# Adding the first experts' output into a copy of x in DRAM instead of into x in SBUF, with three steps of the feed-forward in another order

## The reference

```python
# layer 0, "xattn": a mixture of experts, each token by its id to one of 4 experts
e = min(token_id // (25000 // 4), 3)
y = (silu(h @ ctx[e].T) * (h @ ctx[e].T)) @ ctx[e].T      # h = layernorm(x), ctx[e]: 512 x 512
x = x + tanh(g_xattn[0]) * y
# layer 0, "ffn": block-quantised activations and weights (blocks of 32, shared exponent)
x = x + tanh(g_ffn[0]) * mx_linear(silu(mx_linear(h, w_gate)) * mx_linear(h, w_up), w_down)   # 512 -> 2048 -> 512
# layer 1, "xattn": attention with 8 heads between layernorm(x) and ctx
x = x + tanh(g_xattn[1]) * attention(layernorm(x), ctx)
# layer 1, "ffn": router, 6 of 64 experts of width 192, and a shared expert
x = x + tanh(g_ffn[1]) * moe(layernorm(x))
```

## Time and profile before

| what | us |
|---|---|
| runs of the kernel before | 1041.68, 1046.04, 1039.69 (median 1041.68) |
| the profiled execution: its own time | 1041.68 |
| its span, first to last instruction | 1039.5 |
| experts of layer 0 (20 to 192): PE busy | 165.66 of 172 |
| seam (192 to 214): PE busy, granted clock | 10.49 of 22, 0.82 |
| feed-forward (214 to 408): PE busy | 179.13 of 194 |
| attention (408 to 630): PE busy | 215.39 of 222 |
| routing (630 to 700): PE busy | 65.23 of 70 |
| experts of layer 1 (700 to 1003): PE busy | 298.76 of 303 |

### The profile page before, as it was taken

The page is one execution under the profiler, slowest core; times in us unless marked ns, Lnnn a source line. Parts: engine busy times, 40 slices in busy tenths (PEclk is TensorE's granted clock), DMA queues, the critical chain, the costliest instruction groups (busy, mean ns, idle before and its releaser), DMA issues.

```text
span 1039.5 us, 13635 instructions
## 1 busy us (share of the span) xinstructions
PE 963.3 (93%) x4408; PEld 473.9 (46%) x4430; DVE 623.7 (60%) x1168; ACT 419.0 (40%) x817; POOL 632.1 (61%) x569
## 2 busy tenths in 40 slices
PE   6999999769999998899999999989999999999992
PEld 4454555334444444344444445335554555554530
DVE  5798977268888887677777778962222222222221
ACT  5565656134444444466666654331111111111100
POOL 4698975358888886786667651354554455444430
PEclk9999999989999999899999999999999999999997
DMA  8465431440000001500003405179999999999748
GB/s 274 158 205 195 152 122 71 91 91 1 1 1 1 2 1 41 195 29 21 21 21 86 177 1 203 61 265 296 345 344 338 338 341 341 336 340 333 181 61 186
DMA packets 64788, 162.90 MB, mean 157 GB/s; under 512 B 9760, under 2 KB 9904, under 8 KB 64336
## 3 DMA queue, kind: packets, MB, share of 16 engines
q1 hardware_dynamic: 47360, 116.94, 31.9%
q0 software_dynamic: 17360, 45.10, 18.3%
HBM read 129.67 MB, written 35.48 MB: 159 GB/s over the span
## 4 chain that ended last, share of the span: by engine, by line
PE 55%; POOL 8%; DVE 7%; issue 5%; DMA 3%; ACT 1%; DVEq 0%; POOLq 0%; ACTq 0%
PE PS L1590 15%; PE PS L1609 8%; PE PS L1434 6%; PE PS L1411 6%; PE PS L1422 6%; POOL ARENA L671 4%; PE PS L1579 3%; PE PS L368 3%; PE PS L1376 2%; PE PS L1395 2%; POOL ARENA L677 2%; DMA ARENA<-rows,idx 2%; DVE ARENA L1207 1%; DVE CT L1206 1%; DMA X<-gain 1%
## 5 line engine op out<-in xcount | busy, mean ns | idle before, releaser
L726 POOL TENSOR_TENSOR ARENA<-ARENA 128x512 f32<-128x512 f32 x128 | 133.1, 1061 | 55.5 <-DVE ARENA L1033 55.5
L772 POOL DMA_INDIRECT out<-ARENA,idx x32 | 45.8, 1430 | 127.3 <-DVE ARENA L1239 117.4
L1376 PE MATMUL PS<-SLAB,ARENA 128*128 128x512 bf16 x501 | 116.4, 382 | 3.3 <-ACT ARENA L1731 2.1
L1863 ACT ACTIVATE ARENA<-PS 96x192 f32<-96x192 f32 x64 | 20.9, 326 | 226.5 <-PE PS L1590 149.0
L1239 DVE COPY ARENA<-PS 96x512 f32<-96x512 f32 x64 | 41.1, 682 | 96.6 <-PE PS L1609 96.6
L1770 ACT ACTIVATE ARENA<-PS,ARENA 128x512 f32<-128x512 f32 x128 | 86.7, 682 | 22.8 <-DVE ARENA L1027 19.5
L1027 DVE TENSOR_REDUCE ARENA<-PS 128x2 f32<-128x1024 f32 x64 | 78.2, 1222 | 9.0 <-PE PS L1411 8.9
L1590 PE MATMUL PS<-SLAB,ARENA 128*96 128x384 f32 x240 | 81.0, 490 | 0.0
L1422 PEld LDWEIGHTS PS<-ident,ARENA 128*128 128x128 f32 x512 | 54.8, 141 | 51.1 <-issue 35.8
L1376 PEld LDWEIGHTS PS<-SLAB,ARENA 128*128 128x128 bf16 x512 | 49.6, 99 | 60.8 <-issue 4.8
L677 POOL TENSOR_TENSOR ARENA<-ARENA 128x1024 bf16<-128x1024 fp8e4 x32 | 61.1, 1909 | 24.6 <-DVE ARENA L998 24.5
(11 more groups left out here) (268 smaller groups left out, 1848.2 us busy)
## 6 DMA issues: line engine op xcount, KB each, us to landing
SLAB<-in_L_ffn_w_gate SPq DMA_DIRECT2D x30, 384.0 KB
SLAB<-in_L_ffn_w_up SPq DMA_DIRECT2D x30, 384.0 KB
X<-in_L_ffn_w_down SPq DMA_DIRECT2D x14, 768.0 KB
SLAB<-in_L_ffn_w_down SPq DMA_DIRECT2D x10, 768.0 KB
CT<-in_L_ffn_w_gate SPq DMA_DIRECT2D x16, 384.0 KB
CT<-in_L_ffn_w_up SPq DMA_DIRECT2D x16, 384.0 KB
X<-in_ctx SPq DMA_DIRECT2D x4, 1024.0 KB, 5.4
XNT<-in_L_ffn_w_gate SPq DMA_DIRECT2D x16, 256.0 KB
```

What stands on the lines that cost most here:

```text
L726: last = pool.tensor_tensor(prob[s % 4][:, h, :], prob[s % 4][:, h, :], rec[:, s % 4, h:h + 1].to_broadcast([P, D]), ALU.mult)
L1376: last = pe.matmul(bank(b), QT[:, par, k * P:(k + 1) * P], w[:, k, c * D:(c + 1) * D], start=(k == 0), stop=(k == KD - 1))
```

## The change

**1. Where x and y are added.** The DRAM tensor `gain` becomes `x_sum`. ACT copies x into it, DRAM to DRAM, by four DMAs of 1 MB, issued behind its second `normal_h`. The first scatter waits for these four copies (`x_in`), and every scatter now adds to what the rows of `x_sum` hold. SP's loads of x into `X` in slots 1 to 8 go, and so do POOL's four adding DMAs. Instead SP waits for all scatters and loads `X` tile by tile from `x_sum`, 16 plain DMAs of 256 KB, at most four under way; `enter(i)` waits for its own tile.

**2. POOL's step.** The scale and the offset are computed together (`deviation_x` now has all four operations), so in odd steps the offset's two come ahead of `normal_i(i, 0)` instead of behind it. `normal_h(i + 2)` comes ahead of `back_i(i, 0)` instead of behind it.

**3. DVE's step.** `cast_h` moves from behind the first two products of step i (tile i+1) to the end of the step before (there as tile i+2 of that step), and runs from step 0 on.

```diff
-    gain = nc.dram_tensor("gain", [T + SLOTS * P, D], F32, kind="Internal").ap()
+    x_sum = nc.dram_tensor("x_sum", [T + SLOTS * P, D], F32, kind="Internal").ap()
...
-        PARTS = ((0, 1), (1, 4), (4, 8), (8, NT))
...
                 for j in range(SLOTS):
                     if j in TILED and tile_at(j) + 2 < NT:
                         load_w(tile_at(j) + 2)
-                    if 1 <= j <= NT // 2:
-                        need(sp, c_turned, NT)
-                        sp.dma_start(X[:, 2 * j - 2:2 * j, :], x_v[:, 2 * j - 2:2 * j, :]).then_inc(x_in, 16)
+
+                sp.wait_ge(y_stored[0], 16 * ((SLOTS + 1) // 2))
+                sp.wait_ge(y_stored[1], 16 * (SLOTS // 2))
+                for i in range(NT):
+                    need(sp, yg_in[i % 4], 16 * (i // 4))
+                    sp.dma_start(X[:, i, :], x_sum_v[:, i, :]).then_inc(yg_in[i % 4], 16)
...
                 def scatter(j):
                     if j == 0:
                         pool.wait_ge(target_ready, 1)
+                        pool.wait_ge(x_in, 64)
                     pool.wait_ge(y_out, j + 1)
-                    pool.indirect_dma_start(gain, bass.IndirectOffsetOnAxis(ap=target[:, j:j + 1], axis=0),
-                                            ysb[:, j % 2, :], None).then_inc(y_stored[j % 2], 16)
+                    pool.indirect_dma_start(x_sum, bass.IndirectOffsetOnAxis(ap=target[:, j:j + 1], axis=0),
+                                            ysb[:, j % 2, :], None, compute_op=ALU.add).then_inc(y_stored[j % 2], 16)
...
-                pool.wait_ge(x_in, 16 * (NT // 2))
-                pool.wait_ge(y_stored[0], 16 * ((SLOTS + 1) // 2))
-                pool.wait_ge(y_stored[1], 16 * (SLOTS // 2))
-                for n, (low, high) in enumerate(PARTS):
-                    pool.dma_start(X[:, low:high, :], gain_v[:, low:high, :], accum_op=ALU.add).then_inc(yg_in[n], 16)
...
-                    if i % 2 and i + AHEAD < NT:
-                        offset_x(i + AHEAD - 1, 2)
-                    if live(i, 0):
-                        back_i(i, 0, par)
                     if live(i, 2):
                         normal_h(i + 2)
                     if live(i, 0):
+                        back_i(i, 0, par)
                         normal_i(i, 1, par)
...
                     if live(i, 0):
                         product_i(i, 0, par)
                         product_i(i, 1, par)
-                    if i and live(i, 1):
-                        cast_h(i + 1)
...
                         cast_i(i, 0)
                         product_i(i, 3, par)
                         measure_i(i, 1, par)
+                    if live(i, 2):
+                        cast_h(i + 2)
...
                 normal_h(1)
+                for b in range(B):
+                    act.dma_start(x_sum[b * S:(b + 1) * S, :], x_rows[b * S:(b + 1) * S, :]).then_inc(x_in, 16)
                 silu(0)
```

More of the change, by code:

```diff
@@ L236, in build @@
         x_rows = x.rearrange("b s d -> (b s) d")
-        gain_v = gain[0:T, :].rearrange("(i p) d -> p i d", p=P)
-        PARTS = ((0, 1), (1, 4), (4, 8), (8, NT))
+        x_sum_v = x_sum[0:T, :].rearrange("(i p) d -> p i d", p=P)
         def blocks(a, n=BLK):
@@ L650, in deviation_x @@
                     own.link(pool.tensor_tensor(rs1[:, r:r + n, 0], rs1[:, r:r + n, 0], neg_half[:, 0:1].to_broadcast([P, n]), ALU.pow))
-                def offset_x(i, n):
-                    r = i % R1
                     own.link(pool.tensor_tensor(rs1[:, r:r + n, 1], mv1[:, r:r + n, 0], rs1[:, r:r + n, 0], ALU.mult))
@@ L678, in back_i @@
                                        ALU.mult).then_inc(iq_ready, 1)
-                for i in range(2):
-                    deviation_x(i, 1)
-                    offset_x(i, 1)
+                deviation_x(0, 1)
+                deviation_x(1, 1)
                 normal_h(0)
@@ L685, in _ @@
                 deviation_x(2, 2)
-                offset_x(2, 2)
                 normal_h(1)
@@ L956, in enter @@
                 def enter(i):
-                    dve.wait_ge(yg_in[next(n for n, (low, high) in enumerate(PARTS) if low <= i < high)], 16)
+                    dve.wait_ge(yg_in[i % 4], 16 * (i // 4) + 16)
                     if i >= R1:
```

## The result

| what | us |
|---|---|
| before, median of 9 runs | 1043.61 (1039.69 to 1046.04) |
| after, median of 9 runs | 1051.18 (1048.93 to 1054.16) |
| ratio | 1.0067, 95% interval 1.0056 to 1.0080 |
| the profiled execution after: its own time, its span | 1049.16, 1047.2 |

The changed kernel is 7.0 us slower (0.67%; 5.8 to 8.3), where +2.3 was forecast. Counted from the 1041.68 us that the forecast started from this is 1048.7, just inside its own range of 1039 to 1049, but three times the forecast loss. I compare the two traces at five posts, each the first or last start of one line: the last scatter, the first block maximum of the feed-forward, its first back product, its last clamp, and its last down matmul. The last column is what the stretch since the post before adds.

What follows compares the result with a forecast made beforehand. PE bounds the experts, with a seam and a DVE/POOL feed-forward cycle behind them. From 1041.68 us, -5.5 + 3 + 0.5 + 4.3 = +2.3 gives 1044.0 us; own range 1039 to 1049, 8 in 10 within 1033 to 1057.

Steps and rivals of the forecast that it cites:

- The seam: Last layer 0 scatter to first feed-forward block maximum: maximum at about 202.4 instead of 207.93, -5.5 us, bounds -3.5 and -7.
- The start: Start of layer 0's expert stage: four copies of x delay a weight tile and the first scatter, +3 us, bounds 0 and +13.
- the overlap of the copies with the third tile: Expert stage start: third weight tile, issued alongside the copies, lands at 36 to 38; copies land at 49, bounds 40 and 58.
- rival 3: Expert stage start: copies starve the loads, third weight tile lands only with them (46 to 49), +9 more, 1053; chance 0.16.
- My rule for what a late tile costs: Expert stage start: DVE's rounding had 2.7 us in hand before PE's transposition; DVE 5 late makes PE 2 to 3 late.
- The second wait: Expert stage start: POOL's first scatter waits for all four copies; a scatter 4 us late costs PE 2.
- The other scatters: Expert slots of layer 0: issue 1.41 instead of 1.10 us, hidden but for +0.5 us, bounds 0 and +3.
- The cycle: Feed-forward's two-tile cycle: POOL first at the shared port, odd steps 0.6 us longer, even steps 0.1, +4.3 us in all.
- Rival 1: Feed-forward cycle: DVE gets the shared port first, so the cycle costs 0, time 1039.7; chance 0.22.
- rival 4: Feed-forward cycle: nothing shared between DVE and POOL, gap truly filled, and cheap copies, 1029 to 1031; chance 0.08.
- rival 2: Feed-forward cycle: DVE's small clamp stands behind POOL's big product, +15.6 us instead of +4.3, time 1055; chance 0.12.
- The first step: Feed-forward's first matmuls: at 208.0, still behind PE's low-clock window, so no gain counted for the clock.

Runs made afterwards that it cites:

- experiment 3: Kernel before, with the changed kernel's four copies of x into a DRAM tensor nobody reads, scatters plain: +8.8 us (5.7 to 11.7) against the kernel before.
- 5: Changed kernel with the four copies of x in rows of 2 KB instead of 64 KB: 1.0057 (1.0036 to 1.0077) against the kernel before.
- 6: Changed kernel with POOL's and DVE's old steps, SP issuing the four copies behind the third weight tile: +1.0 us (-1.2 to +3.4) against the kernel before.
- 9: Old steps, DRAM adding, SP issuing two copies behind the third tile, two behind the fourth, first scatter behind the next gather: -5.9 us against the kernel before.
- experiment 2: Kernel before with only the new POOL and DVE steps, plain scatter and adding loads kept: +5.6 us (3.7 to 7.5) against the kernel before.
- experiment 7: Kernel before with small product before back product, offset before big product, or clamp at step's end, each alone: +0.5, +2.8, +16 us; first and third together +2.3.
- Experiment 1: Changed kernel with POOL's and DVE's old steps put back, x and y still added in DRAM: +5.0 us (2.9 to 7.1) against the kernel before.
- (c) alone: Kernel before with only DVE's small clamp (cast_h) moved to the end of the step before: +16 us (11 to 21) against the kernel before.
- with (a): Kernel before with DVE's small clamp at the step's end and POOL's small product ahead of the back product: +2.3 us (0.7 to 4.0) against the kernel before.

## Why the prediction was right, and where it was not

**The seam** (-5.5): -4.8, and the order of events was the forecast one. SP started its loads 3.29 us behind the scatter's issue (205.75 - 202.46) where I took 2.83 from the last stage, the issue took 1.54 instead of 1.41, and tile 0's statistics stood 2.8 behind. From there to the block maximum it took 3.38 us, 3.36 forecast. The first matmul came 16.3 us behind the last scatter, 15.9 forecast.

**The start** (+3, up to +13): +8.8, the term that was mis-sized. The failed step is the overlap of the copies with the third tile, "if the tile lands at 36 to 38". It landed at 42.3, 15 us after its issue, though the copies were done by 40 and not at 49. I had spread the traffic evenly over the loads, and so overrated the copies' own time and underrated what they take from others. What happened is rival 3, the tile landing only behind the copies, with its point of 45 put too late because I took the copies for slow. My rule for what a late tile costs was about right: 10.6 late less 2.7 in hand is 7.9, the first scatter was 9.0 late. It left out PE's clock, which the waits brought down to 0.50 (45 to 50 us). The second wait, on the copies, never came, since they were quick. Experiments 3, 5, 6 and 9 show the cause.

**The other scatters** (+0.5): 0, hidden.

**The cycle** (+4.3): +4.8 between the first back product and the last clamp, 4.9 in experiment 2. POOL was first at the port by the 0.08 us, and the clamp ended 0.55 us behind the small product, as worked out. Two steps take 25.90 where 25.7 was forecast; the 0.2 is in part the big product that now takes longer behind the small clamp (2.03 against 1.92), which I had not priced. Rival 1 (DVE first) and rival 4 (nothing shared) are out, rival 2 is out for this kernel and real in another (experiment 7).

**The first step** (nothing): +1.5 up to the first back product. I had counted no gain for the clock and did not ask for a loss. PE's granted clock was still 1.00 in the 4 us around the block maximum (0.53 before), and 0.52 in the 4 us that start 6 us behind it (0.69 before), where PE runs the first gate and up matmuls; in the 4 us ahead of these it was busy for 1.34 us, 1.00 before. Experiment 1 has 0.50 there and 17.9 us against 16.9, with the old steps. The stretch varies among the other profiles as well, so how much of the 1.5 the change makes is not shown.

**The sum.** By the traces -4.8 + 8.8 + 0 + 1.5 + 4.8 = +10.3 at the last clamp, against +2.3. 2.6 come back later: 1.0 up to the last down matmul, where PE's granted clock is 1.00 and 0.83 from 420 to 440 and was 0.72 and 0.77 from 410 to 430 before, and 1.6 behind it, where no experiment says why. So it is partly luck that the time lies inside my own range of 1039 to 1049: 10.3 would have made 1052. It is within 1% of no change mostly because 1% is 10.4 us.

## What to carry to other kernels

A bulk copy that nobody waits for can still be paid for by whoever shares the DMA engines with it (8.8 us in experiment 3): list the loads that are issued beside and behind it, with the time at which each is wanted, and put the copy in pieces behind the loads that are due first. Ask of every pair of neighbours on DVE and POOL which one will start first and how long the other then waits: a clamp of 0.4 us that starts just behind a product of 1.9 us is a matter of 1.7 us, in each step. One move may need another: (c) alone cost 16 us, with (a) 2. And compare traces at posts between which nothing else varies: the stretch that showed the new steps' 4.8 us repeats within 0.1 us, the one right ahead of it varies by 2.

## What was not expected of the hardware

Behind copies of 64 KB rows in another queue DVE waited 12.4 us for a tile of 0.75 MB, 4.7 with rows of 2 KB, and 1.6 where the same copies stood behind the tile in its own queue. The last indirect DMA that adds took 1.54 us of issue, and SP's loads behind it started after another 3.3 us; 0.96 and 1.8 for a plain one. And one and the same expert stage ended between 192.1 and 196.0 in seven profiles, the two latest with a granted clock of 0.96 from 60 to 100 us, the others of 1.00.
